# Turning the router's logits back, and letting the output leave from the attention's normalised rows: new buffers and a new order in a macaron block of MoE, attention and MoE

## The reference

```python
x = x + 0.5 * ffn(layernorm(x))      # pass "p" in the kernel
x = x + attn(layernorm(x))           # causal window of 64, 16 heads of 16
x = x + 0.5 * ffn(layernorm(x))      # pass "q", the same weights

def ffn(X):                          # E = 8 experts, 2 chosen, hidden 128
    shared = silu(X @ sW1 + sb1) @ sW2 + sb2
    logits = X @ routing_W.T + expert_bias
    act = sqrt(softplus(logits))
    combine = the two largest of act, at their experts, else 0
    return shared + sum_e combine[e] * (silu(X @ rW1[e] + rb1[e]) @ rW2[e] + rb2[e])
```

## Time and profile before

| | |
|---|---|
| median of 3 runs | 1568.83 us (1565.42 to 1570.04) |
| profiled execution, its own time | 1562.98 us |
| its span (first to last instruction) | 1561.1 us |
| mean granted TensorE clock | 0.986 of 2.4 GHz |
| PE, DVE, ACT, POOL busy | 97%, 76%, 72%, 51% |

### The profile page before, as it was taken

How to read it: one execution, slowest core, us unless ns; L and a number is a source line. 1 busy time by engine, 2 the same in 40 slices (tenths; PEclk the granted TensorE clock), 3 DMA queues, 4 the chain that set the end, 5 groups by cost and what they waited for, 6 DMA issues and landing times.

```text
span 1561.1 us, 41431 instructions
## 1 busy us (share of the span) xinstructions
PE 1506.6 (97%) x13969; PEld 1359.6 (87%) x13969; DVE 1186.7 (76%) x4773; ACT 1127.8 (72%) x3416; POOL 790.8 (51%) x794
## 2 busy tenths in 40 slices
PE   7898999999999999999999999999999999999898
PEld 7787889898888989899898988988898898998787
DVE  6857687878868787887878788787878888886554
ACT  5467687877777787787778777777867778686733
POOL 4434455645555464555455455554545554554333
PEclk9998999999999999999999999999999999999899
DMA  3063536344363644545363454546345353635200
GB/s 118 15 203 103 148 120 186 106 137 133 119 170 96 188 119 131 136 125 168 104 187 112 137 130 135 157 119 177 109 138 141 119 159 108 174 108 155 84 28 14
DMA packets 264392, 199.66 MB, mean 128 GB/s; under 512 B 150859, under 2 KB 220918, under 8 KB 264182
## 3 DMA queue, kind: packets, MB, share of 16 engines
q1 hardware_dynamic: 263972, 196.94, 43.8%
q0 software_dynamic: 32, 0.07, 0.0%
q10 hardware_dynamic: 178, 0.02, 0.0%
HBM read 141.86 MB, written 42.43 MB: 118 GB/s over the span
## 4 chain that ended last, share of the span: by engine, by line
PE 59%; DVE 15%; SPq 8%; issue 7%; ACT 5%; DMA 5%; POOL 2%; DVEq 0%; POOLq 0%; ACTq 0%
PE gb L1048 8%; PE gb L1050 8%; PE gb L1049 8%; PE yb L1048 6%; PE yb L1050 5%; PE yb L1049 5%; PE ptb L1121 4%; PE sb_ L1112 4%; SPq L570 4%; PE cxb L1140 3%; ACT pr L717 2%; SPq L565 2%; PE gb L1162 2%; DVE pr L920 1%; DVE ag L998 1%
## 5 line engine op out<-in xcount | busy, mean ns | idle before, releaser
L664 POOL TENSOR_TENSOR gl<-ag,gh 128x512 fp32r<-128x512 f32 x288 | 376.2, 1309 | 267.2 <-ACT gh L762 266.1
L647 POOL TENSOR_TENSOR pr<-pr,rinv 128x512 f32<-128x512 f32 x256 | 274.4, 1074 | 279.5 <-DVE rinv L928 276.6
L717 ACT ACTIVATE pr<-pr,mx 128x128 f32<-128x128 f32 x1024 | 396.4, 391 | 8.7 <-DVE mx L920 6.6
L1048 PE MATMUL yb<-w2h,gh 128*128 128x256 f32 x1152 | 334.7, 291 | 10.5 <-POOL gl L664 10.4
L1050 PE MATMUL yb<-w2l,gh 128*128 128x256 f32 x1152 | 321.7, 279 | 0.0
L1049 PE MATMUL yb<-w2h,gl 128*128 128x256 f32 x1152 | 321.6, 279 | 0.0
L775 ACT ACTIVATE tt<-gb,b1half 128x512 f32<-128x512 f32 x288 | 195.3, 680 | 130.1 <-PE gb L1050 125.9
L920 DVE CUSTOM_DVE_ANT_0 pr<-sb_,mask 128x128 f32<-128x128 f32 x1024 | 235.4, 285 | 36.8 <-issue 25.8
L992 DVE SCALAR_TENSOR_TENSOR ag<-gb,b,gate 128x512 f32<-128x512 f32 x256 | 190.0, 744 | 89.3 <-ACT tt L775 55.7
L1048 PE MATMUL gb<-xh,w1h 128*128 128x512 f32 x576 | 243.2, 422 | 1.7 <-DVE ag L992 1.3
L762 ACT ACTIVATE gh<-ag 128x512 fp32r<-128x512 f32 x288 | 179.9, 625 | 88.3 <-DVE ag L998 68.1
(11 more groups left out here) (154 smaller groups left out, 2827.3 us busy)
## 6 DMA issues: line engine op xcount, KB each, us to landing
gate<-gates_pair SPq DMA_DIRECT2D x240, 256.0 KB, 3.8
ks<-qk_dram SPq DMA_DIRECT2D x256, 128.0 KB, 2.9
qs<-qk_dram SPq DMA_DIRECT2D x512, 64.0 KB, 2.5
qk_dram<-qkh SPq DMA_DIRECT2D x64, 256.0 KB, 2.4
qk_dram<-qkl SPq DMA_DIRECT2D x64, 256.0 KB, 2.7
vb<-va SPq DMA_DIRECT2D x32, 384.0 KB, 6.1
xres<-L_attn_x_dram SPq DMA_DIRECT2D x16, 512.0 KB, 4.6
out_dram<-xres SPq DMA_DIRECT2D x16, 512.0 KB, 4.1
```

What stands on the lines that cost most here:

```text
L647: nc.gpsimd.tensor_tensor(pr[:, k], pr[:, k], rinv[:, k, :].unsqueeze(2).to_broadcast([P, NP, P]), ALU.mult).then_inc(a_pn, 1)
L664: nc.gpsimd.tensor_tensor(gl[:, k, :], ag[:, k, :], gh[:, k, :].bitcast(F32), ALU.subtract).then_inc(f_gl, 1)
L717: nc.scalar.activation(pr[:, k, r, :], pr[:, k, r, :], ACT.Exp, bias=mx[:, k, r:r + 1], scale=-1.0, accum_out=rsum[:, k, r:r + 1]).then_in ...
L1048: nc.tensor.matmul(dst, ah, bh, start=start, stop=False, **kw)
```

## The change

Six things are changed.

1. Logits. `rw` is widened to 128 columns (the router's hi part, its lo part, zeros) and is now the stationary operand: four matmuls of 512 columns make the logits of all rows, experts on partitions. ACT copies them (new step lt) into the free part of `xn`. A new step M turns them back and adds hi and lo in one: four plain fp32 matmuls with the copied logits stationary and `fold` (two identities of 8 on top of each other) streamed. DVE's first add goes. The lo part of the router now also meets the lo part of the activations.
2. Output. T of pass q writes to `axn`, and OUT sends `axn`. The wait of aR for the output goes; T waits for the transposes of `axn` of the image two ahead, and aN2 for the output of the image three before.
3. The last pass. For image 15, pass q keeps its residual in `xin` in place of `x2` and uses the p half of `xh` and `xl`.
4. Raw weights are loaded through `gate`, `x2` and `axn`; Wz has no wait any more.
5. `HEAD`, `TAIL` and `ORDER` are all made anew. Fillings: 73 in the head, 15 in the tail.
6. Semaphore counts follow.

One line of each kind of table, as an example:

```diff
-ph14=15 qt8=14 qgh7=14 qgh8=14 ph15=15 cth1=15 qN2=15 qxh0=15 qxh1=15 qt0=15 qen=15 qgh0=15 qct=15 qt1=15
+ex15=15 ph13=15 qen=14 ph14=15 ph15=15 cth1=15 qcr=14 qct=14 qt1=14 qt2=14 qN2=15 qgh1=14 qt3=14 qgh2=14
```

The rest of the diff, with context left out:

```diff
-        rw = sb("rw", [P, KC, 2 * E], F32R)
+        rw = sb("rw", [P, KC, P], F32R)
+        fold = sb("fold", [P, E])
+        lgt = xn_flat[:, 2 * NT * E * E:]
-        raw = va[:, :, :, :].rearrange("p h b d -> p (h b d)")
+        raw = gate[:, :, :].rearrange("p g l -> p (g l)")
...
+        def res(b):
+            return xin[b % NXI] if b == B - 1 else x2
+        def half(s, b):
+            return 0 if s[0] == "p" or b == B - 1 else 1
...
                 elif s == "OUT":
                     sp.wait_ge(f_res, 2 * nth("q", b) + 2)
-                    sp.dma_start(out[b].rearrange("(t p) d -> p t d", p=P), x2).then_inc(x_out, 16)
+                    sp.dma_start(out[b].rearrange("(t p) d -> p t d", p=P), axn[:, :, :]).then_inc(x_out, 16)
...
+            select(fold[:], ALU.not_equal, 1.0, 0, [[-1, E]], 1)
+            select(fold[:], ALU.not_equal, 1.0, -E, [[-1, E]], 1)
...
                 if s == "Wz":
                     nc.gpsimd.memset(qs[:].bitcast(F32), 0.0).then_inc(w_zero, 1)
-                    pool.wait_ge(w_lo, max(lo_done("1r"), lo_done("1t")))
                     nc.gpsimd.memset(va[:], 0.0).then_inc(w_zero, 1)
...
                 elif s == "aN2":
                     act.wait_ge(a_rstd, 4 * b + 4)
                     wait(act, a_xt, 2 * b)
+                    wait(act, x_out, 16 * (b - 2))
+                    if b == 0:
+                        act.wait_ge(w_lo, lo_done("vo"))
...
                     act.wait_ge(f_xt, 2 * n + c + 1)
-                    if b > 0:
+                    if half(s, b) == 0 and s[0] == "q":
+                        act.wait_ge(f_h, NE * nth("p", b) + NE)
+                    elif b > 0:
                         act.wait_ge(f_h, NE * nth(s, b - 1) + NE)
...
+                elif s[1:] == "lt":
+                    n = nth(s, b)
+                    act.wait_ge(f_lgt, n + 1)
+                    nc.scalar.activation(lgt, bank(s[0] + "L", b), ACT.Copy).then_inc(f_lgs, 1)
...
-                acc = psum[:, 0:NT * 2 * E].rearrange("p (t e) -> p t e", t=NT)
-                op(nc.vector.tensor_tensor(lg[:], acc[:, :, E:2 * E], ebias[:].unsqueeze(1).to_broadcast([P, NT, E]),
-                                           ALU.add))
-                op(nc.vector.tensor_tensor(lg[:], acc[:, :, 0:E], lg[:], ALU.add))
+                op(nc.vector.tensor_tensor(lg[:], psum[:, 0:NT * E].rearrange("p (t e) -> p t e", t=NT),
+                                           ebias[:].unsqueeze(1).to_broadcast([P, NT, E]), ALU.add))
...
                 elif s[:2] == "aR":
                     h = int(s[2])
                     dve.wait_ge(a_o, 2 * b + h + 1)
-                    wait(dve, x_out, 16 * b)
-                    nc.vector.tensor_tensor(x2[:, 2 * h:2 * h + 2, :],
+                    nc.vector.tensor_tensor(res(b)[:, 2 * h:2 * h + 2, :],
...
                     else:
-                        rd, wr = x2, x2
+                        rd, wr = res(b), axn
+                        dve.wait_ge(a_xt, min(2 * b + 6, 2 * B))
+                        if b >= B - 2:
+                            dve.wait_ge(x_out, 16 * b)
                     dve.wait_ge(f_y, NE * n + NE)
...
                 elif s[1] == "L":
-                    for t in range(NT):
-                        ts = slice(t * P, (t + 1) * P)
-                        for k in range(KC):
-                            nc.tensor.matmul(tile[:, 2 * E * t:2 * E * t + 2 * E], xh[:, q, k, ts], rw[:, k, :],
-                                             start=(k == 0), stop=False, skip_group_check=True)
-                            mm = nc.tensor.matmul(tile[:, 2 * E * t:2 * E * t + E], xl[:, q, k, ts], rw[:, k, 0:E],
-                                                  start=False, stop=(k == KC - 1), skip_group_check=True)
+                    for k in range(KC):
+                        nc.tensor.matmul(tile, rw[:, k, :], xh[:, q, k, :], start=(k == 0), stop=False)
+                        mm = nc.tensor.matmul(tile, rw[:, k, :], xl[:, q, k, :], start=False, stop=(k == KC - 1))
+                    mm.then_inc(f_lgt, 1)
+                elif s[1] == "M":
+                    n = nth(s, b)
+                    pe.wait_ge(f_lgs, n + 1)
+                    for t in range(NT):
+                        mm = nc.tensor.matmul(bank(s[0] + "L", b)[:, E * t:E * t + E], lgt[:, t * P:(t + 1) * P], fold[:],
+                                              start=True, stop=True, skip_group_check=True)
                     mm.then_inc(f_lg, 1)
```

More of the change, by code:

```diff
@@ L235 @@
[L235 to L239 removed]
+ST10=11 psp4=12 psp5=12 psp6=12 psp7=12 ST11=11 qG1=10 qsp0=10 qsp1=10 qsp2=10 qsp3=10 LX=14 qsp4=10 qsp5=10
@@ L240 @@
+psp6=15 psp7=15 ST11=14 qG1=13 qsp0=13 qsp1=13 qsp2=13 qsp3=13 qsp4=13 qsp5=13 qsp6=13 qsp7=13 QW0=15
+ST00=15 ST01=15 QW1=15 OUT=13 ST10=15 VS=15 ST11=15 qG1=14 qsp0=14 qsp1=14 qsp2=14 qsp3=14 qsp4=14 qsp5=14
+qsp6=14 qsp7=14 OUT=14 OUT=15
 """,
@@ L519, in load @@
                 else:
+                    if k == "qk":
+                        sp.wait_ge(w_smt, 1)
                     for c, w in enumerate((wq, wk) if k == "qk" else (wv, wo)):
-                        sp.dma_start(x1[0 if k == "qk" else 1][:, 2 * c:2 * c + 2, :],
+                        sp.dma_start((x2 if k == "qk" else axn)[:, 2 * c:2 * c + 2, :],
                                      w.rearrange("(k p) n -> p k n", p=P)).then_inc(done, 16)
@@ L598, in _ @@
             nc.gpsimd.memset(sel32[:], 0.0).then_inc(w_const, 1)
-            made = [9]
+            nc.gpsimd.memset(fold[:], 0.0).then_inc(w_const, 1)
+            nc.gpsimd.memset(rw[:, :, 2 * E:].bitcast(F32), 0.0).then_inc(w_const, 1)
+            made = [11]
             pool.wait_ge(w_const, made[0])
@@ L732, in step @@
                     wait(act, f_g1, 16 * ns(s, b))
-                    src = xin[b % NXI] if s[0] == "p" else x2
+                    src = xin[b % NXI] if s[0] == "p" else res(b)
                     for t in range(NT):
@@ L765, in step @@
                     act.wait_ge(f_gpe, E * (s[0] == "q") + m + 1)
+                    if n == 0 and m == 0:
+                        act.wait_ge(w_lo, max(lo_done("1r"), lo_done("1t")))
                     wait(act, f_a, NE * (n - 1) + m + 6 if m < 4 else NE * n + m - 2)
@@ L845, in ranks @@
             def ranks(n):
-                op = chain(n, 7)
+                op = chain(n, 6)
                 lj = lg[:].unsqueeze(2).to_broadcast([P, NT, E, E])
@@ L940, in step @@
                     wait(dve, f_rstd, 4 * n)
-                    stats(xin[b % NXI] if s[0] == "p" else x2, stat, mv, f_stat, 8 * n)
+                    stats(xin[b % NXI] if s[0] == "p" else res(b), stat, mv, f_stat, 8 * n)
                 elif s[1:3] == "xl":
-                    n, c, q = nth(s, b), int(s[3]), "pq".index(s[0])
+                    n, c, q = nth(s, b), int(s[3]), half(s, b)
                     dve.wait_ge(f_xh, 2 * n + c + 1)
@@ L1152, in step @@
                 elif s[1] == "L":
-                    n, q = nth(s, b), "pq".index(s[0])
+                    n, q = nth(s, b), half(s, b)
                     weights("rw", n == 0)
@@ L1182, in step @@
                 elif s[1] == "H":
-                    e, n, q = int(s[2]), nth(s, b), "pq".index(s[0])
+                    e, n, q = int(s[2]), nth(s, b), half(s, b)
                     weights("1s" if e == 0 else "1r" if e == 1 else "1t", n == 0 and e in (0, 1, 1 + E // 2))
```

390 lines of the change are left out of this document (195 added, 195 removed).

## The result

The changed kernel took 1604.86 us (median of 4 runs, 1602.06 to 1608.54) against 1567.12 us for the kernel before: 1.0243 times as long, 95% interval 1.021 to 1.0277. The forecast was 1552 us with a range up to 1567, so it was wrong in sign. The profiled execution has a span of 1604.7 us, 43.6 more than in the earlier trace rows.

A forecast was written before the change was run, and what follows sets the result against it. TensorE, busy 97% of 1561.1 us, was taken as the bound, with gains only from less middle work or at the ends. Logits +5, tail -12.6, head -9 sum to -16.6 us: 1552 us, range 1535 to 1567.

The forecast's parts named there:

- the one on SyncE: SyncE's queue: the output's send, now ahead of the shift of the values, delays nothing; priced at nothing.
- the middle's new order: Middle stretch of 1257.4 us: the new order changes nothing, 0, with -6 to +8 us.
- The logits: TensorE's router logits, 32 passes: 1.83 us a pass for 1.70, +5 us in all, bounds +2 and +9.
- The last image: Image 15, first score matmul to last value step: less TensorE work beside it, 51 us, -21.8 us.
- the term of -12.6: Tail together: -21.8 us in image 15's attention stretch, +9.2 us behind the last projection; bounds -19.6 and +0.4.
- The start: Head of the kernel: fewer fillings and an earlier GpSimd clearing, -9 us, bounds 0 and -17.
- (1): Head: fillings before the first transposes shrink from 24 to 8, -1 us.
- (3): Head: 20 fillings fewer, 4.6 us, where the order has other work, -3 us.
- M waited 0.3 us for ACT: Rival, pass q: M waits 0.95 us a pass for ACT's evacuation, +28 us, 1580; chance 0.08.
- the attention chain: Rival: image 15's stretch stays at 64 us, its steps following one another; tail 0, 1565; chance 0.11.
- the overlap that doesn't come about: Rival: image 15's pass q shares buffers with image 14 and must wait; counted with the chain rival, chance 0.11.
- the dear fp32: Rival: plain fp32 costs double to load in the logits' turning back, +29 for +5 us, 1576; chance 0.03.

The follow-up runs named there:

- e5: Kernel before, with only the shift of the values moved ahead of the gate row's write and broadcasts in SP's repeated order: 1610.7 us.
- e1: Changed kernel with the gate row's write and first two broadcasts put back ahead of the shift of the values: 1593.9 us.
- e2: Changed kernel with the gate row's write directly behind ST01 and three broadcasts ahead of the shift of the values: 1588.0 us.
- e4: Changed kernel with the DVE's row maxima of the fifth score block ahead of the gated activations of experts 1 and 2: 1589.5 us.
- e6: Kernel of e2 with the next image's statistics moved back behind the gated activations of expert 3: 1580.2 us.
- e10: Changed kernel with all five engines' repeated orders and the logits of the kernel before, keeping new ends and buffers: 1565.8 us.
- e8: Changed kernel with the logits of the kernel before alone, without copy and fold: 1606.3 us.
- e9: Kernel of e6 with the logits of the kernel before, without copy and fold: 1584.9 us.
- e11: Kernel of e10 with the new logits, copy and fold set into its orders, DVE's additions a little later: 1617.8 us.
- e13: Kernel of e10 with the gate row's write early in repeated orders and written-out ends, statistics later in the ends: 1557.9 us.
- e3: Changed kernel with eleven filling steps ahead of the fourth H of images 4 to 12: 1597.7 us.

## Why the prediction was wrong

**The step that failed** is the one on SyncE: "OUT now stands ahead of VS; it waits for a DVE step that stands ahead of VS's own releaser, so nothing." OUT stood ahead of VS before as well (801.92 and 807.14 in the queue above); what had moved in the repeated order was the gate row, from ahead of VS to behind it, and the forecast has no term for that. With it fell "the middle's new order I take at 0, -6 to +8". Measured: +46.9 over nine periods. e5 shows that this move alone can cost 43 us in the old order; e1 and e2 show that in the changed kernel its share is 11 to 17, since there the DVE's new order (statistics in front of the gated activations, these in front of the maxima: e4, e6) stands in the same loop. That TensorE asks for the bank sooner (15.0 us behind the scores for 16.1) is in the trace, but no run moved it alone. With all repeated orders taken back the loss of the nine periods is 3.8 us (e10).

**The logits**: forecast +5 with a lower bound of +2, measured 1.74 for 1.70 a pass, +1.3 us (M took 0.81 for the forecast's 0.92), and nothing in e8 and e9. Small, as forecast, but the forecast charged only TensorE and left out that the copy and M lengthen the gates' path (e11).

The page "TensorE: Matmul & The Clock Gate" of the Trainium skill gives fast loading of weights only to types other than fp32 (section on weight-path modes). M's plain fp32 records stand 0.10 us apart, no dearer than the 0.106 of the earlier trace rows, so the trace doesn't bear out a price for it here; whether the fp32r operands of those rows had the fast loading themselves, no run shows.

**The last image**: the mechanism was right. From its first scores to its last value step (1481.80 to 1531.00) 49.2 us, forecast 51, with ACT busy for 41.25, forecast 42:

```profile
1481.80:1531.00 49.20, 39.48 (x516) 34.92 (x514) 30.87 (x201) 41.25 (x161) 19.86 (x22) 0.87 0.40 105
1531.00:1604.70 73.70, 65.66 (x436) 58.82 (x436) 39.62 (x84) 31.25 (x54) 26.66 (x23) 0.94 0.13 44
...
1531.00:1539.20 8.20, 6.96 (x61) 6.73 (x62) 2.24 (x8) 1.66 (x3) 1.12 (x1) 0.52 0.15 48
1539.20:1604.70 65.50, 58.70 (x377) 52.09 (x375) 37.38 (x76) 29.59 (x51) 25.54 (x22) 0.99 0.13 43
```

From the last value step to the end it took 73.7 us for 60.3, +13.4. Behind the last projection (1539.20) these are 65.5 us, forecast 64.5. The stretch with the projection itself, to which the forecast gave no change, took 8.2 us for 5.0, at a clock of 0.52. Fillings fell from 15.39 us to 3.99. Together that is -10.2 us for the term of -12.6. But the tail begins earlier than image 15: in the three images ahead +9.1 came back, the same late gates in the written-out tables. Mended (e13), these two stretches give 6.4 of the 12.6.

**The start**: in the window from 40 to 60 us PE was busy 19.7 us at a clock of 1.00, where the earlier trace rows have 16.12 at 0.83; this step was right. Yet the first scores of image 0 came at 96.8 for 100.0, and those of image 3 2.2 us sooner (by -2.8 to 2.2 in the seven profiles with this start), for the -9 forecast. So what this term gave can't be told from the scatter. One part was counted twice: the cut from 24 to 8 fillings in (1) is 16 of the "20 fillings fewer" that (3) prices again. Where the rest went isn't shown; 1.66 us of the 19.7 are fillings themselves.

**The rivals**: M waited 0.3 us for ACT in the whole run, so that one is out; the attention chain (64 us) and the overlap that doesn't come about are out with the 49.2 us above, the dear fp32 with M's 0.81. None of the rivals was the true one. The rival on the slow side that was missing is the plainest: a DMA on the gates' path moved behind another on the same queue.

## What to carry to other kernels

A table of orders has to be read on the queue of DMAs as carefully as on the bounding engine: for each step that another step now stands ahead of, ask what the one ahead waits for and who waits for the one behind. Find the loop with the least slack (here logits, gates, row, broadcast, DVE, bank) and price every edit by what it does to that loop, since an edit that is free in one order can be dear in another (the new logits: e9 and e11). Find by the buffers which step really waits: my e5 looked at H4, and the bank was H3's. And cut both traces at marks that enclose the same work before speaking of a gain at an end.

## What the runs showed that I had not expected

Two issues of 0.64 and 0.62 us moved ahead of the gate row in SP's queue cost 43 us over the run (e5), since the first of them waited 2.8 us, the row behind them took 5.1 instead of 3.9 us to its broadcast, and the bank had only 1.7 us to spare (all three in image 8). With 20.4 us of waits of H filled, the granted clock of the nine periods was 0.99 for 0.98, and they took 7.3 us less (e3).
